# Moving two of three dense products of a graph layer into its edge stage, on one Trainium2 core

## What is computed

```
m   = x[src] * rel[edge_type]
m   = concat(m[:half] @ W_in, m[half:] @ W_out)
deg = segment_sum(ones, dst); norm = 1 / max(deg, 1)
agg = segment_sum(m * norm[dst], dst)
h   = x + res * tanh(agg + x @ W_loop + b)
```

## Time and profile before

| what | before |
|---|---|
| median of three runs | 3220.51 us |
| span of the profiled execution | 3183.3 us |
| instructions | 55393 |
| PE / DVE / ACT / POOL busy | 87 / 72 / 59 / 61% of the span |
| HBM read, written | 263.90, 45.48 MB |

### The profile page before, as it was taken

The page is one execution under the profiler, slowest core; times in us unless marked ns, Lnnn a source line. Parts: engine busy times, 40 slices in busy tenths (PEclk is TensorE's granted clock), DMA queues, the critical chain, the costliest instruction groups (busy, mean ns, idle before and its releaser), DMA issues. The chain is left out here.

```text
span 3183.3 us, 55393 instructions
## 1 busy us (share of the span) xinstructions
PE 2759.1 (87%) x20688; PEld 2587.3 (81%) x20688; DVE 2303.9 (72%) x3258; ACT 1865.5 (59%) x3179; POOL 1952.0 (61%) x2129
## 2 busy tenths in 40 slices
PE   4888888888888888797888888888888887997998
PEld 3888888888888888796877887878777786997998
DVE  6777777777677777896777777777777776995665
ACT  6556665555555555585555555555555554785444
POOL 6666666666666666455666666666666664892223
PEclk9999989999999999899999999999999999998999
DMA  8333333333333333353333333333333333452221
GB/s 259 119 90 89 89 89 90 89 89 90 88 89 90 90 88 90 92 164 104 90 90 90 89 90 92 88 90 90 89 89 92 88 90 98 136 158 90 69 67 64
DMA packets 162458, 312.57 MB, mean 98 GB/s; under 512 B 34061, under 2 KB 95309, under 8 KB 162229
## 3 DMA queue, kind: packets, MB, share of 16 engines
q0 software_dynamic: 79872, 218.21, 23.8%
q1 hardware_dynamic: 81120, 89.89, 8.8%
q10 hardware_dynamic: 1237, 1.41, 0.2%
HBM read 263.90 MB, written 45.48 MB: 97 GB/s over the span
## 5 line engine op out<-in xcount | busy, mean ns | idle before, releaser
L740 PE MATMUL edge_rg<-edge_rel_hi,edge_hot 128*128 128x256 f32 x6656 | 1551.7, 293 | 86.6 <-issue 63.0
L740 PE MATMUL edge_rg<-edge_rel_lo,edge_hot 128*128 128x256 f32 x4992 | 1312.3, 289 | 60.0 <-issue 58.9
L740 PEld LDWEIGHTS edge_rg<-edge_rel_hi,edge_hot 128*128 128x128 f32 x6656 | 1219.6, 197 | 143.7 <-issue 92.2
L548 ACT ACTIVATE edge_hot<-edge_typ,minus_type 128x512 fp32r<-128x512 f32 x832 | 526.8, 685 | 935.9 <-DMA dense_prev<-emb_t 383.9
L740 PEld LDWEIGHTS edge_rg<-edge_rel_lo,edge_hot 128*128 128x128 f32 x4992 | 983.1, 197 | 70.0 <-issue 68.5
L623 DVE TENSOR_TENSOR edge_m_lo<-edge_rg,edge_m_hi 128x1024 fp32r<-128x1024 f32 x416 | 509.3, 1224 | 241.3 <-ACT edge_m_hi L541 127.7
L604 DVE TENSOR_SCALAR edge_hot<-edge_typ,type_of 128x512 fp32r<-128x512 f32 x832 | 582.3, 741 | 12.4 <-ACT edge_hot L548 8.7
L753 PE MATMUL edge_small<-edge_m_hi,edge_sel 128*128 128x258 f32 x1664 | 458.1, 306 | 96.3 <-DVE edge_m_lo L623 90.7
L530 POOL DMA_INDIRECT edge_xg<-emb,src x416 | 399.0, 959 | 225.9 <-issue 96.2
L530 POOL DMA_INDIRECT work<-h,src x416 | 400.7, 963 | 221.9 <-issue 101.9
L530 POOL DMA_INDIRECT edge_xg<-h,src x416 | 400.2, 962 | 216.2 <-issue 102.8
(11 more groups left out here) (183 smaller groups left out, 3933.9 us busy)
## 6 DMA issues: line engine op xcount, KB each, us to landing
work<-emb,src POOLq DMA_INDIRECT x416
edge_xg<-emb,src POOLq DMA_INDIRECT x416
work<-h,src POOLq DMA_INDIRECT x416
edge_xg<-h,src POOLq DMA_INDIRECT x416
set_x_rows<-in_x SPq DMA_DIRECT2D x25, 256.0 KB, 3.9
emb<-set_e_rows SPq DMA_DIRECT2D x25, 256.0 KB, 2.9
emb_t<-acc SPq DMA_DIRECT2D x5, 1280.0 KB
dense_prev<-emb_t SPq DMA_DIRECT2D x25, 256.0 KB, 2.7
```

What stands on the lines that cost most here:

```text
L548: act.activation(hot[:, q % 2, c], typ[q % 2][:], ACT.Abs, bias=K["minus_type"][:, c:c + 1]).then_inc(distances, 1)
L740: ins = pe.matmul(rg[q % 2][:, t, :], hot[:, q % 2, c, t * P:(t + 1) * P], part[:, c, :], start=(c == 0 and part is rel_hi), stop=(c == FULL))
```

## The change

- The product with W_loop and the left half's product with W_in are made inside the edge stages of both layers. Chunks 0 to 24 of the previous nodes begin at groups 6, 10, ... 102, those of the left sums at groups 110, 114, ... 206 (`begins`). A chunk costs ACT a high part three groups ahead and DVE a low part in place two groups ahead; PE makes 12 matmuls into `made`, which is bank 0 of `small`: six (`first_columns`) behind relation_rows of turn g, after a wait for the sums last added from that bank, and six (`last_columns`) behind one_window of turn g+1. ACT copies the result over the chunk in `acc` (`chunk_copy`), and the window product that next uses the bank (group g-2, in turn g+2) waits for the copy.
- Loop products go to DRAM as `loop_t` (25 stores by SP); ACT then clears the chunk three groups later. Left products stay in `acc`.
- Both layers now store the previous nodes' columns in five transfers at the start of the edge stage, and DVE's low part waits for them. SP loads W_loop there, and W_in after the last chunk of the first kind.
- The dense stages keep the right half: 12 matmuls a chunk. DVE adds the left product (`join`), multiplies by the inverse degrees, which PE spreads over the partitions from one row by a float32 matmul with K = 1 (`widen`), the loop product is loaded and added (POOL in layer 0, DVE in layer 1), then tanh and residual. In layer 0 the residual writes to the right area of `acc`, which replaces the store of `h_t`, and only the left half is cleared. The inverse is taken once, after a transfer of the one row of degrees to 128 partitions and back. In layer 1 the bias mu_b comes in by four one-row matmuls instead of POOL's addition.
- `acc` is laid out `[128, 2, nodes]`, a zero of one column replaces the tile of zeros, and PE's dense stage of layer 0 is unrolled.

```
+FIRST_LOOP = 6
+FIRST_LEFT = 110
+PACE = 4
...
+        made = small[0][:].rearrange("p (o n) -> p o n", o=DC)
...
+        def begins(g):
+            for stage, start in enumerate((FIRST_LOOP, FIRST_LEFT)):
+                if (g - start) % PACE == 0 and 0 <= (g - start) // PACE < CHUNKS:
+                    return stage * CHUNKS + (g - start) // PACE
+            return None
...
+            def chunk_high(n):
+                act.copy(part_hi[:], chunk_of(K["acc"], n)).then_inc(part_high, 1)
+            def chunk_copy(n):
+                act.wait_ge(made_done, n + 1)
+                act.copy(chunk_of(K["acc"], n), made).then_inc(made_copied, 1)
...
+            def side_work(g, q, i):
+                if g == 2:
+                    split_own(0)
+                if g == FIRST_LEFT - 4:
+                    split_own(1)
+                n = begins(g + 3)
+                if n is not None:
+                    if n == CHUNKS:
+                        act.wait_ge(added, PAIRS // 2)
+                    chunk_high(n)
+                n = begins(g)
+                if n is not None:
+                    chunk_copy(n)
+                    if n == CHUNKS - 1:
+                        act.sem_inc(own_free, 1)
+                n = begins(g - 3)
+                if n is not None and n < CHUNKS:
+                    clear(n)
...
-                over_groups(act, (0, later(distance)), (2, high), (0, later(one_hot)), (3, copy_sums), (0, clear_one))
+                over_groups(act, (0, later(distance)), (2, high), (0, later(one_hot)), (3, copy_sums), (0, side_work))
...
+            def chunk_product(n, o):
+                ps, cols = made[:, o], slice(o * P, (o + 1) * P)
+                if o == 0:
+                    pe.wait_ge(part_low, n + 1)
+                    pe.wait_ge(own_lo, n // CHUNKS + 1)
+                for k in range(DC):
+                    ins = product(pe, ps, [w_own[:, v, k, cols] for v in range(2)],
+                                  [part_hi[:, k], chunk_of(K["acc_r"], n)[:, k]], k == 0, k == DC - 1)
+                if o == DC - 1:
+                    ins.then_inc(made_done, 1)
...
+                def first_columns(g, q, i):
+                    n = begins(g)
+                    if n is not None:
+                        pe.wait_ge(added, g // 2 - 2)
+                        chunk_product(n, 0)
+                def last_columns(g, q, i):
+                    n = begins(g - 1)
+                    if n is not None:
+                        chunk_product(n, 1)
                 def one_window(g, q, i):
+                    n = begins(g + 2)
+                    if n is not None:
+                        pe.wait_ge(made_copied, n + 1)
                     pe.wait_ge(lo_done, g + 1)
...
-                over_groups(pe, (4, one_window), (2, relation_rows), (0, spread_later), (4, turn_over))
+                over_groups(pe, (4, one_window), (0, last_columns), (2, relation_rows), (0, first_columns),
+                            (0, spread_later), (4, turn_over))
...
+            def join(c, b, n, d, m):
+                dve.wait_ge(lin_done, c + 1)
+                dve.tensor_tensor(z[:, d, :, at], lin[b][:, :, at], left(c, width(c)), ALU.add).then_inc(joined, 1)
+            def scale(c, b, n, d, m):
+                dve.wait_ge(inv_done, c + 1)
+                dve.tensor_tensor(z[:, d, :, at], z[:, d, :, at],
+                                  inv[b][:, at].unsqueeze(1).to_broadcast([P, DC, width(c)]), ALU.mult).then_inc(scaled, 1)
...
             if first:
-                over_chunks(dve, (1, weights_low), (3, residual), (1, scaled_low), (0, scale), deep=DEEP)
+                over_chunks(dve, (0, weights_low), (0, invert), (3, residual), (1, scale), (0, join), deep=DEEP)
             else:
-                over_chunks(dve, (0, weights_low), (4, moments), (2, residual), (0, scaled_low), (1, combine),
-                            (6, columns_low), deep=DEEP)
+                over_chunks(dve, (0, weights_low), (0, bias_parts), (1, scale), (3, residual), (0, join),
+                            (5, moments), (1, add_loop), (7, columns_low), deep=DEEP)
...
-                over_chunks(pe, (0, linear), (1, to_rows), deep=DEEP)
+                over_chunks(pe, (0, linear), (0, widen), (4, to_rows), deep=DEEP, rolled=False)
```

More of the change, by code:

```diff
@@ L154, in product, with half_of, blank @@
     return pe.matmul(out, a[0], b[0], start=False, stop=last)
-def columns(K, chunks):
-    return K["acc"][:, ACC_W:, :].rearrange("p n k -> p (n k)").rearrange("p (c k n) -> p c k n", k=DC, n=CHUNK)[:, chunks]
+def half_of(area, h, c, n=CHUNK):
+    return area[:, :, ds(h * ACC_W + c * CHUNK, n)]
+def blank(K, *shape):
+    v = K["zero"][:]
+    for _ in shape[1:]:
+        v = v.unsqueeze(2)
+    return v.to_broadcast([P, *shape])
 def phase_setup(nc, K, x, dst_tiles, src_tiles, res, emb, types):
@@ L427, in over_groups, with phase_edges @@
         turn(STEPS + t // GROUPS_IN_RING, t % GROUPS_IN_RING)
[L430 removed]
+def phase_edges(nc, K, layer, nodes, rel, nodes_t, loop_t, own, matrices, dst_tiles):
     first = layer == 0
@@ L512, in _ @@
             sp.wait_ge(matrices_in, 16 * len(matrices))
-            if first:
-                sp.wait_ge(columns_out, 16 * CHUNKS // 5)
+            for k in range(CHUNKS // 5):
+                sp.wait_ge(columns_out[k], 16)
+            sp.wait_ge(loop_out, 16 * CHUNKS)
         @block.gpsimd
@@ L852, in phase_dense @@
         if first:
-            clamped = s.sem("clamped")
-            normed = s.sem("normed")
             cleared = s.sem("cleared")
-            t_out = [s.sem(f"t_out{k}") for k in range(2)]
+            spread = NODES_PAD // P
+            counts = s.sb("counts", [P, spread])
+            counts_in = s.sem("counts_in")
+            inverted = s.sem("inverted")
+            inv_in = s.sem("inv_in")
         else:
@@ new lines, in invert @@
+            def invert(c, *place):
+                if isinstance(c, int) and c == 0:
+                    dve.wait_ge(counts_in, 16)
+                    dve.tensor_scalar(counts[:], counts[:], 1.0, None, ALU.max).then_inc(inverted, 1)
+                    dve.wait_ge(inverted, 1)
+                    dve.reciprocal(counts[:], counts[:]).then_inc(inverted, 1)
+            def join(c, b, n, d, m):
+                dve.wait_ge(lin_done, c + 1)
+                wait_past(dve, h_done if first else h_lo, c + 1 - DEEP)
+                at = slice(0, width(c))
+                dve.tensor_tensor(z[:, d, :, at], lin[b][:, :, at], left(c, width(c)), ALU.add).then_inc(joined, 1)
```

416 lines of the change are left out of this document (219 added, 197 removed).

## The result

The changed kernel takes 3346.68 us (median of 4 runs, 3340.45 to 3352.17), the kernel before 3220.7 us beside it: ratio 1.0394, 95% interval 1.0377 to 1.0412, so 126 us **slower**. The forecast was 3252 us with a range of 3180 to 3310.

A forecast was written before the change was run, and what follows sets the result against it. Edge stages were taken as paced by TensorE's work, stalls and waits, not gathers; the second dense stage by DVE. +87 (edges) - 39 - 17 (dense stages) = +31 us on 3220.5 gave 3252 us, range 3180 to 3310.

The forecast's parts named there:

- -17 us forecast: Second dense stage: DVE stays the bound, a chunk falls from 6.36 to 5.75 us; 17 us saved (5 to 25).
- Rival C: Dense stages give little: TensorE falls to 1.2 GHz in the first; both save 22, not 56; 3285 us; chance 0.08.
- +87 forecast: Both edge stages: added matmuls and longer stalls, less covered waits, net 0.87 us times 100 passes, +87 us (0 to 165).
- minimum of 18.6 us: Edge stages: a pass (four groups) where TensorE waits for nothing, from two turns of 9.32 us; actual pass 23.6 us.
- the other 5 us: Edge-stage pass beyond 18.6 us: stalls 1.8, waits for DVE and ACT 1.2 to 1.8, some 2 only implied.
- I take half of 1.2 to 1.8: 0.7 us: Edge stages: part of TensorE's waits for DVE and ACT that the added products would cover, 0.7 us a pass.
- sign for the gathers: Edge stages: the forecast would be wrong if gathers set the pace; then passes would not move at all.
- net 0.87 us a chunk: Edge stages, one chunk per pass: 1.43 us of matmuls plus 0.14 of stalls less 0.70 of covered waits.
- Rival A: Edge stages: products fall into TensorE's waits and cost 20 us in all; kernel 3185 us, faster; chance 0.30.
- Rival B: Edge stages: ACT's copy delays DVE's low part and the next window product; 165 us, kernel 3329 us; chance 0.10.
- 0.14 us a pass for a longer stream: Edge stages: TensorE's issue stalls of 1.8 us a pass grow by 8% with the instruction stream; 14 us in all.
- -39 forecast: First dense stage: a chunk falls from 4.78 to 3.1 us, bound by ACT; 39 us saved (28 to 48).

The follow-up runs named there:

- e1_order: Changed kernel, DVE's second dense stage reordered: moments, residual, columns_low first, join last; 3182.63 us beside 3182.75 of the kernel before (ratio 1.0005).
- e5: Kernel before, second dense stage: DVE's moments moved behind residual and scaled_low, waiting for the same turn's linear product; 3343.24 us against 3182.75.
- e6_order2: Changed kernel, DVE's second dense stage ordered moments, residual, scale, add_loop, columns_low, join; 3196.92 us beside 3218.42 of the kernel before (ratio 0.9934).
- e2: Changed kernel plus 36 useless matmuls per chunk in the second dense stage, where TensorE waits; order unchanged; 3256.93 us.
- e8: Kernel before, with three of four gathers in each group after the fourth; 2710.89 us beside 3182.51 of the kernel before.
- r2_before: Kernel before, unaltered, run and profiled again; 3185.02 us.
- e3: Changed kernel with 2 of 12 matmuls per chunk product in the edge stages; edge stages 2540.8 us against 2561.7 in the changed kernel.
- e11: e6_order2 with three of four gathers in each group after the fourth, as in e8; edge stages 1062.5 and 1056.0 us.
- after: First profile of the changed kernel, unaltered (3346.68 us measured); edge stages 1275.8 and 1281.6 us, second dense stage 323.3.
- e1b_moments: Changed kernel with only moments moved first in DVE's turn of the second dense stage, the rest as in the change; 3230.62 us.
- e10: e6_order2 with each loop product stored four times; edge stages 1274.7 and 1285.5 us against 1279.8 and 1281.9 in e6_order2.
- e9: e6_order2 with gathers of group g released earlier, by the message of group g-4; 3361.03 us, ratio 1.0568 to the kernel before.

## Why the prediction was wrong

**The second dense stage is the step that failed: -17 us forecast, +141 measured.** The sentence was "DVE stays the bound, with 0.2 us of idle as now: 5.75 us". The sentence adds up work and leaves out the order. It doesn't ask what stands in DVE's turn behind the new stage join, which waits for the product of the same turn, and who needs that in the same turn; the prediction did ask so of ACT's copy in the edge stages. e1_order shows that the order is worth 127 of the 141 us here, and e5 that such a ring alone costs 160 us in a kernel without any of the change's operations.

With the work in another order, e6_order2, a chunk took 5.8 us and the stage 10.6 us less than before, within the 5 to 25 that I gave, but that is in part luck: the sum of 5.5 us for DVE kept its residual at 1.62 us, and it took 0.77. In the 120 us from 2740 to 2860 DVE was busy for 96 and TensorE for 113, at a granted clock of 0.91, so it wasn't DVE that bound the stage.

**Rival C had the fallen clock in the wrong stage and without its cause.** It let the clock fall to 1.2 GHz in the first dense stage because TensorE is no longer full there; that stage had 1.00. The clock fell in the second one, for some 53 us (e2), where the ring made TensorE wait.

**The edge stages: +87 forecast, +27 measured.** A pass grew from 23.7 to 24.0 us, where 24.5 was forecast. The step that failed is in the reading of the bound: "That is near, and it is not the bound: POOL waits for others in the rest." POOL issues a gather every 1.25 us where nothing holds it, one in 1.48 us in the mean, so its issues alone are not the bound; but the gathers are: with three of four a pass falls from 23.7 to 19.03 us (e8). I had the minimum of 18.6 us from the unhindered turns and explained the other 5 us by stalls, waits and hidden waits without a row that said who was late. DVE's 3.18 us for something remote in the earlier trace rows was a message that waited. In r2_before such waits make 134.0 of 900 us, 3.5 us a pass, twice the 1.2 to 1.8 us that the sum had for TensorE's waits, and in e8 they are gone. So the step "I take half of 1.2 to 1.8: 0.7 us" was mis-sized: with +27 us for 100 passes, all but some 0.3 of the 1.43 us was covered. The prediction's own sign for the gathers, passes that do not move at all, was too strict: they moved by 0.3 us. e3 gives 21 us back for ten of the twelve matmuls.

That the forecast's net 0.87 us a chunk is near the 0.99 of e11 is a coincidence, since TensorE has no waits there to cover the rest. Rival A, products in the waits, gave 20 us for the edge stages and was nearly right there, for a reason that it didn't name. Rival B's price, 165 us, did not come; TensorE's waits above don't show the copy.

The 0.14 us a pass for a longer stream, 14 us in all, did not show: "issue" ahead of the relation rows grew by 4 us in both layers together, and the same relation rows had none in e8. The Trainium skill (Runtime: NRT & Kernel Launch, section Instruction fetch mechanics) says that crossing a block is mostly hidden, and e8's 0.1 us in 900 agrees. What the "issue" stalls of the full kernel are stays open; they go with the gathers.

The start of the second layer was costed at nothing, or 10 us if the gathers had to wait: its first five turns took 27.1 us before and 31.5 to 32.3 with the five column stores (after, e1_order, e1b_moments, e2_filler), as the first layer's did in both kernels (32.0). That is some 4.6 of the 27 us; that the stores are the cause was not tried.

**The first dense stage: -39 forecast, -48 measured** (-42 to -48 over the profiles of this code), the end of its range. A chunk takes 3.1 us as forecast (24 to 25 of POOL's additions in the 75 us of the stretch above), but the bound is POOL with 67.4 us busy, for which TensorE waits, not ACT with 59.5 (groups by line of the same stretch):

```profile
L1127 POOL TENSOR_TENSOR dense_z<-dense_z,dense_loop 128x512 f32<-128x512 f32 (+1 forms) x25 | 40.1, 1606 | 1.0 <-DVE dense_z L1190 1.0
L1119 POOL TENSOR_TENSOR dense_parts<-acc,dense_parts 128x512 fp32r<-128x512 f32 x23 | 29.3, 1273 | 7.6 <-ACT dense_parts L1318 6.6 <-PE dense_lin L157 0.2
...
L1205 DVE SCALAR_TENSOR_TENSOR acc<-dense_z,res,dense_prev 128x512 f32 (+2 forms) x25 | 24.2, 970 | 6.7 <-ACT dense_z L1348 6.7
```

POOL's addition took 1.61 us where its low part took 1.27, DVE's residual 0.97 where it had 0.74. The Trainium skill (SBUF — State Buffer, section SBUF: two separate sides) has a DVE operation with two SBUF inputs and a GpSimd operation lock each other out of a shared port. Both durations agree with it, though POOL's addition is not the same operation as its low part and no run takes one of the two engines away. The price that the prediction put on it, 5 us of the gain by DVE's turn, did not come: DVE had 21 of 75 us to spare. Nor does POOL's busy share fix the residual's time, as the prediction had it: it took 0.77 us in e6_order2 beside a POOL that was busy for 87 of 120 us.

**The sum** was put on 3220.5 us with 37.2 us around the span, where 2 us lie. That didn't move the forecast's difference. But the plain difference of the first two profiles, 155 us, is 29 more than was measured.

## What to carry to other kernels

Where engines run a software pipeline in a fixed order, busy sums give the floor and not the time: for each stage that is added or moved, write down which turn of which engine it waits for, what stands behind it in its own turn, and whether the engine it waits for needs any of that in the same turn. If so, the pipeline is one ring, whatever the lags say, and the cure is the order: stages that feed others first, the one that waits for the newest product last.

Before pricing work put on a busy engine, find what sets the pace: if idle time can't be assigned, take a little away from the suspect (here one gather of four) and see whether the loop shortens.

## What was not expected of the hardware

- Gathers of 128 rows of 1 KB, issued at 1.25 us each, came through at one in 1.48 us at best beside TensorE's work, at 90 GB/s. Stores beside them, 131 GB/s in all, did not slow them (e10); more of them in flight did (1.62 us each, used 20.7 instead of 10 to 11 us after the last issue, e9). What limits them stays open.
- 36 useless matmuls a chunk made the second dense stage 53 us shorter: the granted clock was 1.00 in place of 0.57 (e2).
